# Band attention with its FFN on one core: values transposed by DMA, four engines' orders rewritten

## The reference

```python
xn  = layernorm(x)                                  # x: (8, 1024, 512)
Q, K, V = xn @ Wq + bq, xn @ Wk + bk, xn @ Wv + bv  # 16 heads of 64
scores  = Q K^T; scores = where(|i - j| <= 64, scores, 0.0)
attn    = softmax(scores, axis=-1)                  # over all 1024 columns
out = attn @ V @ Wo + bo
s = xn @ Win + bin_; h = relu(s[..., None] * W1 + b1)      # 64 units, 16 inner
g = sum(h * W2, -1) + b2; ffn = g @ Wout + bout
x + out + ffn
```

## Time and profile before

| | |
|---|---|
| median of 3 runs | 2254.79 us (2249.35 to 2255.46) |
| profiled execution | 2249.37 us, span 2247.6 us |
| mean granted TensorE clock | 0.953 |
| PE, PEld busy | 1994.0, 1110.4 us |
| DVE, ACT, POOL busy | 1754.1, 1473.2, 1399.4 us |
| DMA transposes | 512, all from SP's queue |

### The profile page before, as it was taken

One profiled execution on the slowest core, in us unless ns is written; L12 is line 12 of the kernel. 1 busy time (PEld: TensorE's weight loads), 2 busy tenths in 40 slices (PEclk: granted clock), 3 DMA queues, 4 the chain that ended last, 5 costly groups with the idle time before them and its releaser, 6 DMA issues.

```text
span 2247.6 us, 41992 instructions
## 1 busy us (share of the span) xinstructions
PE 1994.0 (89%) x14211; PEld 1110.4 (49%) x14211; DVE 1754.1 (78%) x4579; ACT 1473.2 (66%) x3961; POOL 1399.4 (62%) x1504
## 2 busy tenths in 40 slices
PE   7778888899889998899998999989989899889996
PEld 4444454555445554555454555545554555444553
DVE  5899877897678876888767887688776897677875
ACT  4767666667657675667666675657756667657664
POOL 3645547566577665667647665667747566577565
PEclk8889899999999999999999999999999999999998
DMA  3554435545365443555436545365445555354455
GB/s 120 129 125 98 104 91 116 138 104 113 71 139 131 103 97 78 141 127 112 95 76 148 113 102 109 72 173 108 96 80 115 138 105 113 70 138 96 91 102 118
DMA packets 610422, 247.01 MB, mean 110 GB/s; under 512 B 547336, under 2 KB 559648, under 8 KB 610208
## 3 DMA queue, kind: packets, MB, share of 16 engines
q1 hardware_dynamic: 610160, 244.30, 49.3%
q10 hardware_dynamic: 48, 0.01, 0.0%
HBM read 84.84 MB, written 25.17 MB: 49 GB/s over the span
## 4 chain that ended last, share of the span: by engine, by line
PE 36%; DVE 24%; ACT 20%; POOL 14%; issue 6%; DMA 0%; SPq 0%; ACTq 0%; DVEq 0%; POOLq 0%
PE ps L1128 16%; ACT probs L528 9%; POOL probs L386 8%; PE ps L1114 6%; ACT p_hi L584 6%; PE ps L1143 5%; DVE xn L901 4%; DVE acc L883 4%; DVE probs L851 4%; PE ps L1184 4%; POOL oT_lo L393 2%; POOL p_lo L399 2%; DVE row_l L863 1%; ACT qT_hi L576 1%; DVE vT L936 1%
## 5 line engine op out<-in xcount | busy, mean ns | idle before, releaser
L1128 PE MATMUL ps<-xT_hi,w_split 128*128 128x512 f16 x3072 | 985.7, 386 | 6.7 <-DVE xT_lo L739 6.4
L386 POOL TENSOR_SCALAR probs<-probs,inv_l,neg_e 128x256 f32<-128x256 f32 x1024 | 591.3, 597 | 290.4 <-DVE neg_e L870 290.2
L399 POOL TENSOR_TENSOR p_lo<-probs,p_hi 128x1024 f16<-128x1024 f32 x256 | 550.4, 2161 | 85.6 <-ACT p_hi L584 85.5
L1128 PE MATMUL ps<-xT_lo,w_split 128*128 128x512 f16 x1536 | 591.0, 385 | 0.0
L528 ACT ACTIVATE probs<-probs,neg_max 128x256 f32<-128x256 f32 x1024 | 505.2, 498 | 23.7 <-DVE neg_max L858 23.1
L1128 PEld LDWEIGHTS ps<-xT_hi,w_split 128*128 128x128 f16 x3072 | 304.2, 99 | 386.0 <-issue 30.4
L851 DVE CUSTOM_DVE_ANT_0 probs<-ps,mask,unit_s 128x256 f32<-128x256 f32 x1024 | 432.9, 477 | 43.8 <-PE ps L1114 43.8
L393 POOL TENSOR_TENSOR oT_lo<-o_sum,oT_hi 128x512 f16<-128x512 f32 x128 | 162.4, 1269 | 435.3 <-ACT o_sum L596 435.3
L584 ACT ACTIVATE p_hi<-probs 128x1024 f16<-128x1024 f32 x256 | 269.1, 1051 | 215.7 <-POOL probs L386 212.4
L883 DVE SCALAR_TENSOR_TENSOR acc<-ps,unit_o,acc 128x512 f32<-128x512 f32 x512 | 358.5, 740 | 18.6 <-PE ps L1143 18.5
L1143 PE MATMUL ps<-wo_split,oT_hi 128*128 128x512 f16 x1024 | 318.3, 394 | 53.8 <-DVE xT_lo L739 28.3
(11 more groups left out here) (119 smaller groups left out, 2969.2 us busy)
## 6 DMA issues: line engine op xcount, KB each, us to landing
w_split<-w_kept SPq DMA_DIRECT2D x168, 256.0 KB, 3.0
acc<-in_L_attn_x SPq DMA_DIRECT2D x14, 1024.0 KB, 7.0
out_x<-acc SPq DMA_DIRECT2D x14, 1024.0 KB, 5.3
wo_split<-wo_kept SPq DMA_DIRECT2D x56, 256.0 KB, 2.9
w_kept<-w_split SPq DMA_DIRECT2D x24, 256.0 KB, 2.4
pT_hi<-p_hi SPq DMA_TRANSPOSE x256, 3.1
pT_lo<-p_lo SPq DMA_TRANSPOSE x256, 3.3
acc<-in_L_attn_x SPq DMA_DIRECT2D x4, 512.0 KB, 5.6
```

The costliest lines, as they stand in the source:

```text
L386: pool.tensor_scalar(probs[:, h, t], probs[:, h, t], inv_l[:, c:c + 1], neg_e[:, c:c + 1], ALU.mult, ALU.add).then_inc(normed, 1)
L399: pool.tensor_tensor(p_split[lo][:, h, tiles], probs[:, h, tiles], p_split[hi][:, h, tiles], ALU.subtract).then_inc(p_lo, 1)
L1128: last = pe.matmul(dst[:], w[wp][:, i, c], xT[xp][:, c, half * LINE:half * LINE + LINE], start=(c == 0 and a == 0), stop=(c == KC - 1 and ...
```

## The change

V is no longer transposed on PE. ScalarE's `values_high` makes the fp16 high half of vT with the mean off (v_neg as its bias) into v_split, VectorE's `values_low` the low half, and SP's `transpose_values` brings both into v by two DMA transposes. The centring in place and the vT banks are gone, v is laid out by halves, and `value_means` also writes v_back. The orders of PE, DVE, ACT, POOL and SP change, the four low halves on POOL are four instructions each, and the banks are given out anew. The diff's core (eight columns of indentation left out):

```diff
 vT = sb("vT", [P, N])
-v = sb("v", [P, 2, T, 2, 2, D], F16)
+v_split = [sb(f"v_{part}", [P, N], F16) for part in ("hi", "lo")]
+v = sb("v", [P, 2, 2, T, 2, D], F16)
...
-V_BANK, VT_BANK = (3, 1), (6, 7)
+V_BANK = (6, 1)
 QK_BANK = (7, 2, 2, 3)
-OUT_BANK = (7, 0, 4, 5, 7, 0, 4, 5)
-PV_BANK = (6, 5)
-XT_BANK = (6, 0, 4, 1, 7, 0, 1, 6)
+OUT_BANK = (7, 0, 4, 5, 1, 0, 4, 5)
+PV_BANK = (6, 3)
+XT_BANK = (6, 7, 4, 5, 0, 1, 4, 5)
 FIRST_XT_BANK = (4, 5, 0, 2)
-FFN_IN_BANK = (6, 1)
-FFN_OUT_BANK = ((6, 3), (0, 1), (6, 4), (6, 3))
+FFN_IN_BANK = (6, 7)
+FFN_OUT_BANK = ((6, 3), (0, 1), (6, 7), (6, 3))
...
+TOP_BANK, LAST_TOP_BANK, FIRST_TOP_BANK, TOP_COLUMN = 1, 3, (1, 6), 32
 WARM_UP = 28
...
+    def transpose_values(n):
+        if n >= 2:
+            sp.wait_ge(pv_done, 2 * n - 2)
+        for part, ready in ((hi, v_hi), (lo, v_lo)):
+            sp.wait_ge(ready, n + 1)
+            sp.dma_start_transpose(v[:, n % 2, part].rearrange("p t h d -> p t (h d)"), v_split[part][:]) \
+                .then_inc(v_got, 16)
...
             load_x(b + 1, k - 2)
         if attend:
             transpose_weights(j, 0, 0, hi)
+            transpose_weights(j, 0, 0, lo)
             transpose_weights(j, 0, 1, hi)
-            transpose_weights(j, 0, 0, lo)
-            transpose_weights(j, 0, 1, lo)
         if k == 1 and b > 0 and proj:
             store(b - 1, 0)
         if proj:
             next_weights(V_)
+        if attend:
+            transpose_weights(j, 1, 0, hi)
+            transpose_weights(j, 0, 1, lo)
+        if proj:
             next_weights(Q_)
         if attend:
-            transpose_weights(j, 1, 0, hi)
             transpose_weights(j, 1, 1, hi)
         if proj:
...
         if attend:
             transpose_weights(j, 1, 0, lo)
             transpose_weights(j, 1, 1, lo)
+        if proj:
+            transpose_values(n)
         if n == PAIRS - 1:
...
         def weights_low(half, h):
-            tiles = slice(4 * half, 4 * half + 4)
             pool.wait_ge(p_hi, 4 * j + 2 * half + h + 1)
-            pool.tensor_tensor(p_split[lo][:, h, tiles], probs[:, h, tiles], p_split[hi][:, h, tiles],
-                               ALU.subtract).then_inc(p_lo, 1)
+            for t in tiles_of(half):
+                last = pool.tensor_tensor(p_split[lo][:, h, t], probs[:, h, t], p_split[hi][:, h, t],
+                                          ALU.subtract)
+            last.then_inc(p_lo, 1)
         def add_biases(p):
...
             normalise_weights(0)
-        if n <= PAIRS:
+        if n < PAIRS:
             inverse_root(tops_of_step(n), top_ready, scaled_in(n), root_ready)
         if attend:
             weights_low(0, 0)
-            weights_low(0, 1)
         if out_proj:
             output_low(1)
         if k == 0 and proj:
...
         if n == 0:
             add_biases(2)
             add_biases(3)
+        if k == 5 and not last:
+            inverse_deviation(slice(0, T), b + 3)
+        if attend:
+            normalise_weights(1)
+            weights_low(0, 1)
+            weights_low(1, 0)
+            weights_low(1, 1)
+        if n == PAIRS:
+            inverse_root(tops_of_step(n), top_ready, scaled_in(n), root_ready)
         if k == 1 and proj and b > 0:
             add_biases(2)
-        if k == 5 and not last:
-            inverse_deviation(slice(0, T), b + 3)
-        if attend:
-            normalise_weights(1)
-            weights_low(1, 0)
-            weights_low(1, 1)
-        if k == 1 and proj and b > 0:
             add_biases(3)
...
-        def values_high(i):
-            act.wait_ge(v_T, 2 * n + i + 1)
-            act.activation(v[:, n % 2, 4 * i:4 * i + 4, :, hi, :].rearrange("p c h d -> p (c h) d"),
-                           ps[VT_BANK[i]][:].rearrange("p (c d) -> p c d", d=D), ACT.Copy).then_inc(v_hi, 1)
+        def values_high():
+            act.wait_ge(v_stat, 3 * n + 3)
+            if n > 0:
+                act.wait_ge(v_got, 32 * n)
+            act.activation(v_split[hi][:], vT[:], ACT.Identity, bias=v_neg[:]).then_inc(v_hi, 1)
...
             for i in (Q_, K_, V_):
                 weights_top(n + 1, i)
+        hidden_high(0)
+        if ffn and k == 5:
+            network_high()
...
         if ffn and k == 0:
             x_high(b, 5)
-            x_high(b, 6)
         if attend:
             exps(3)
         if ffn and k == 0:
+            x_high(b, 6)
             x_high(b, 7)
-        if proj:
-            value_lines(0)
-        if attend:
-            weights_high(0, 1)
         if out_proj:
             weighted_sums(1)
-        hidden_high(0)
-        if ffn and k == 5:
-            network_high()
+        if proj:
+            value_lines(0)
+        if attend:
+            weights_high(0, 1)
         if ln_next and k == 6:
             normalise(b + 1, 2)
             normalise(b + 1, 3)
+        hidden_high(1)
         if proj:
             value_lines(1)
         if ln_next and k == 7:
             x_high(b + 1, 0)
         if ffn and k == 0:
             gather(0)
-        hidden_high(1)
+        hidden_high(2)
         if split_next:
             split_high(n + 1, V_)
         if ln_next and k == 7:
             x_high(b + 1, 1)
+        if proj:
+            values_high()
         if attend:
             weights_high(1, 0)
         if proj:
             qk_high(2)
         if split_next:
             split_high(n + 1, Q_)
-        hidden_high(2)
-        if ln_next and k == 6:
-            normalise(b + 1, 4)
-            normalise(b + 1, 5)
+        hidden_high(3)
         if attend:
...
             split_high(n + 1, K_)
-        if proj:
-            values_high(0)
-            values_high(1)
         if ln_next and k == 5:
...
         if ln_next and k == 7:
             normalise(b + 1, 6)
             normalise(b + 1, 7)
-        hidden_high(3)
...
-        def centre_values():
+        def value_means():
             dve.wait_ge(v_in, 2 * n + 2)
             dve.tensor_tensor(v_mean[:, 0:1], v_sums[:, 0:1], v_sums[:, 1:2], ALU.add).then_inc(v_stat, 1)
             dve.wait_ge(v_stat, 3 * n + 1)
             dve.tensor_tensor(v_mean[:, 1:2], v_mean[:, 0:1], v_sums[:, 2:3], ALU.add).then_inc(v_stat, 1)
             dve.wait_ge(v_stat, 3 * n + 2)
-            dve.tensor_scalar(v_new[:], v_mean[:, 1:2], 1.0 / N, None, ALU.mult).then_inc(v_stat, 1)
+            if n > 0:
+                dve.wait_ge(v_hi, n)
+            dve.tensor_scalar(v_neg[:], v_mean[:, 1:2], -1.0 / N, None, ALU.mult).then_inc(v_stat, 1)
             dve.wait_ge(v_stat, 3 * n + 3)
-            dve.tensor_scalar(vT[:], vT[:], v_new[:], None, ALU.subtract).then_inc(v_centered, 1)
-        def values_low(i):
-            part = [v[:, n % 2, 4 * i:4 * i + 4, :, p, :].rearrange("p c h d -> p (c h) d") for p in (hi, lo)]
-            dve.wait_ge(v_hi, 2 * n + i + 1)
-            dve.tensor_tensor(part[lo], ps[VT_BANK[i]][:].rearrange("p (c d) -> p c d", d=D), part[hi],
-                              ALU.subtract).then_inc(v_lo, 1)
+            if out_proj:
+                dve.wait_ge(o_summed, 2 * o + 2)
+            if n < PAIRS:
+                dve.wait_ge(bias_ready, k + 1)
+            dve.tensor_tensor(v_back[:, n % 2:n % 2 + 1], bias_scaled[:, V_, k:k + 1], v_neg[:], ALU.subtract) \
+                .then_inc(v_back_ready, 1)
+        def values_low():
+            dve.wait_ge(v_hi, n + 1)
+            dve.scalar_tensor_tensor(v_split[lo][:], vT[:], v_neg[:], v_split[hi][:],
+                                     ALU.add, ALU.subtract).then_inc(v_lo, 1)
...
+        if o > 0:
+            add_output(6, o - 1)
+            add_output(7, o - 1)
+        if 0 < j <= PAIRS:
+            split_output_low(j - 1)
+        if attend:
             mask_scores(1)
             mask_scores(2)
             denominators(0)
...
             qk_low(1)
-        if n <= PAIRS:
+        if ffn and k == 0:
+            x_low(b, 5)
+        if n < PAIRS:
             read_tops(tops_of_step(n), TOP_BANK, top_sum, scaled_in(n), top_ready)
         if ffn and k == 0:
-            x_low(b, 5)
             x_low(b, 6)
+        if ffn and k == 5:
+            network_low()
+        hidden_unit(0)
         row_statistics(0)
         if ln_next and k == 5:
             mean_and_variance(range(T), T * b + 2 * T, b + 3)
-        if attend:
-            denominators(1)
-        if n <= PAIRS:
-            step_scales(n)
         if ffn and k == 0:
             x_low(b, 7)
+        if attend:
...
             add_output(0)
             add_output(1)
         if ffn and k == 7:
             add_network(3)
-        hidden_unit(0)
         row_statistics(1)
-        if ffn and k == 5:
-            network_low()
+        if out_proj:
+            add_output(2)
...
         if ffn and k == 6:
-            add_network(0)
-        if out_proj:
-            add_output(2)
-            add_output(3)
-        if proj:
-            centre_values()
+            add_network(1)
+        if proj:
```

(94 more changed lines are left out.)

143 lines of the change are left out of this document (63 added, 80 removed).

## The result

The changed kernel takes 2305.85 us (median of four runs, 2302.93 to 2308.8) beside 2254.23 for the kernel before: a ratio of 1.0233, 95% interval 1.0211 to 1.0255. It is 2.3% slower, where 9% faster was forecast. The profiled execution has a span of 2301.2 us at a mean granted clock of 0.923. Every time given here is of a fast execution, except that the profile of e9_past_waits is of one of 2340.79 us in the slow state, which is left out of its times.

What follows compares the result with a forecast made beforehand. The prediction took middle steps as bound by PE plus a few waits, the first batch by DVE. Gains of 152 us (six middle batches), 33 (first) and 17 (last), together 202, gave 2050 us, range 1975 to 2165.

Steps and rivals of the forecast that it cites:

- plus 0.3 for each step of DVE waiting for POOL: Term of the middle-batch sum: DVE waits for POOL 0.3 us in each step, 2.4 us a batch.
- rival three: POOL's 11 us run of norm(1) and three low halves holds DVE's SBUF operations: 288 us, time 2335; chance 0.09.
- PE's 69 us: Value transposes and their waits leave PE: 1.08 us for each of 64 steps, 69 us.
- PE's idle time: Sign that the forecast is right: PE busy near 1920 us with some 120 us idle.
- 244.5 us: Forecast length of a middle batch's eight steps, for 269.8 us before: a gain of 25.3, times six 152.
- DVE's 80 us: Centring and two PSUM subtractions go, one 1.4 us update comes: about 80 us of DVE freed, 1.25 a step.
- Rival one: POOL shuts DVE's value sums out and values_high waits: 2.8 us every second step, 90 us, time 2140; chance 0.14.
- POOL's quarters: Low halves as four instructions of 0.56 us each on POOL, adding 0.4 us a step.
- a gain of some 33: First batch, bound by DVE: steps of 34.5 us against 39.2 for five, about 3 for each other three.
- Orders of PE: PE's new order removes most of the 4.9 us idle in k=7 and 3.9 in k=0; signs near 33 and 36.
- The remaining wait for kT_lo: At each step's end PE waits 0.35 us for kT_lo, whatever else is freed; 2.8 us a middle batch.
- Rival two: Late low halves on POOL delay PE's first weighted sums: 1.6 us a step, 102 us, time 2150; chance 0.14.

Runs made afterwards that it cites:

- e9_past_waits: e1_gaps with every GpSimd wait moved to the instruction before the last, so it is already met: ratio 1.0251 to the kernel before.
- e1_gaps: Changed kernel with GpSimd waiting for its own last instruction ahead of each low-half quarter and each bias instruction: 2126.22 us, 0.9451 of the kernel before.
- e7_before_gaps: Kernel before with only GpSimd's own-semaphore waits ahead of each whole low half and each bias instruction: 2185.36 us, ratio 0.9684.
- e5_gaps_keepq: Changed kernel with both edits, the GpSimd waits of e1_gaps and the SP order of e4_keepq: 2101.46 us, ratio 0.9315.
- e8_before_quarters: Kernel before with only each low half cut into four instructions, no waits between: 2348.3 us, ratio 1.0396.
- e11_gaps_early_swap: e10_gaps_early with SP's transpose of low half (0,1) also ahead of the (1,0) high one: 2164.75 us, ratio 0.9622.
- e12_pairs: e5_gaps_keepq with each low half in two pieces of 128x512 instead of four, a wait between each two: 2086.05 us, ratio 0.9267.
- e4_keepq: Changed kernel with SP issuing Q's store and next load ahead of transposes (1,0,hi) and (0,1,lo) in the first batch: 2273.46 us, ratio 1.0105.
- A and D: Two losses the experiments tested: A, DVE's SBUF instructions held through POOL's unbroken run (e1_gaps); D, SP's order in the first batch (e4_keepq).
- e10_gaps_early: e5_gaps_keepq with weights_low(0,1) moved back ahead of norm(1): 2165.97 us, ratio 0.964.
- e6_wgaps_keepq: e5_gaps_keepq with each low half one whole instruction instead of four quarters: 2135.0 us, ratio 0.9468.

## Why the prediction was wrong

**The step that failed** is the term "plus 0.3 for each step of DVE waiting for POOL", with the reason given against rival three: that most operations find a way between norm's short instructions, "and the low halves now come in such lengths". The same sum had put POOL's norm and low halves in one unbroken run of 11 us, and rival three named its place, hidden_unit(2) ahead of qk_low(3). It was given 0.09. Held over 2 us, DVE had 30 instructions in the kernel before (117 us), 67 after (278 us), none in e1_gaps. What e1_gaps gave back is 180 us, 2.8 us a step where 0.3 was taken: short of the 4.5 that the rival was priced at and near its point of decision, 3.2. A microsecond held is not a microsecond of time: 278 us of holds taken away gave 180, and 117 in the kernel before gave 70 (e7_before_gaps).

Of the 256 us between 2050 and 2306, then, 180 are this term, 25 SP's order (e5_gaps_keepq against e1_gaps), and 51 are left, 56 by the profiled executions. By the steps of e5_gaps_keepq they lie in the 48 middle ones (1503.6 us, where the sum had 1619.9 less 152) with 36, in the first batch with 18 and in the last with 5; the start and the tail give 3 back.

What misled was a reading of the median in the earlier trace rows: 0.80 for the centring beside a longest of 5.03. It was taken as what one meets between short instructions. It shows how DVE fares beside norm; at the joint of two low halves the row below it, 4.21 us of L399 x2, already showed a joint at which DVE didn't get in. e8_before_quarters is the test that would have settled it: more joints without a true wait are only a longer run.

**How long a hold lasts.** The 5.03 us was held against the sentence of the Trainium skill, "SBUF — State Buffer", section "SBUF: two separate sides", that the shared pair is locked for one whole instruction. The measurements go further: 11.93 us through more than ten instructions. They agree with the page where POOL truly waits between two (e1_gaps, at most 1.17 us in the same line), and at nearly all joints of norm's instructions (below).

**PE's 69 us**: busy time fell by 59.4 at a granted clock that fell from 0.953 to 0.923, while PE's idle time grew from 253.6 to 366.6 us. With the long waits gone (e1_gaps, clock 0.971) it is 117.6 less than before, part of it the clock's. In e11_gaps_early_swap, at 0.949, nearly the clock of before, it is 71.8 less. Right in size.

**PE's idle time** was to fall to some 120 us. It is 249.6 in e1_gaps, 222.3 in e5_gaps_keepq and 205.4 in e12_pairs, and 219.8 in the kernel before with waits alone (e7_before_gaps). So even undisturbed the change takes work off PE and hardly any waiting; that the middle batches come near their 244.5 us all the same (250.6 in e5_gaps_keepq) is in part a higher clock, 0.978 for 0.953, which the sum had not counted on. That part is luck.

**DVE's 80 us**: 104.5 more instead. In e1_gaps, where nothing is held long, busy time is 162.7 below the kernel before, twice what was taken, as the old holds went too. values_low was taken at 1.4 us:

```profile
L965 DVE SCALAR_TENSOR_TENSOR v_lo<-vT,v_neg,v_hi x64: 1268/1628/5293, 47.6 to 2255.7; 128x1024 f16<-128x1024 f32 x64
```

Its shortest, 1.27, is the lower bound, its longest, 5.29, a little past the upper one; in e1_gaps the median is 1296 ns. The size was right, the company wrong.

**ACT** was costed at nothing beside the wait for value_means. values_high takes 1.15 us (1.05 taken), and its wait for v_neg is 138.4 us, 73.5 in e5_gaps_keepq. Rival one (priced 90) is not what makes it: only 3 of the 64 first value sums are over 2 us longer than the shortest (7 us in all), and half of the wait is there where nothing is held long. Mostly ScalarE waits because DVE comes to the sums late; what that costs in time no run shows.

**POOL's quarters**: 0.56 us taken. In the run above they take 7.56 / 12 = 0.63, on average 0.69. All low halves together went from 550.4 to 672.1 us, 1.9 a step where 0.4 was taken. norm(1), to start 2.7 us sooner, starts 1.2 us sooner in k=4 (20.5 us into the step at the median, 21.7 before).

**DMA and SP.** The values' transposes were rightly free: issue 1.28 us, landing 3.3 at the median, nobody waits. But the sum looked only at what is read from SP's queue late, not at what must be written early: w_kept's store in the first batch. It cost some 30 us (e4_keepq), on a batch from which a gain of some 33 was expected (five steps by 4.7 and 9).

**Orders of PE.** k=7 "near 33" came (33.4), and k=0 at 33.6, better than the 36. k=4, forecast at 28 to 29, took 31.4 in the batch shown and up to 36.2 in others; in e1_gaps it is at 29.2. The remaining wait for kT_lo, taken as 0.35 us a step, has a median of 0.41 us in e1_gaps outside the first batch (33.6 us in 55 times), and 62.2 us in 8 times within it.

**Rival two** was right but hidden. With A and D gone PE waits 85.7 us for the late low halves, near the 102 it was priced at, and more than the 51 us between e5_gaps_keepq's 2101 and the 2050 forecast. Whether it makes that gap is not shown: the edit that takes the wait away costs more than it gives (e10_gaps_early), and pairs take part of it and make the wait for kT_lo longer.

Set against the kernel before with waits (2185), the change as made but for the joints (2126) is worth 59 us (52 by the ratios), and with SP's order 84. But the first has whole low halves and the others quarters. With whole ones in both, and SP's order (e6_wgaps_keepq, 2135.0), it is 50 us. So its value is real, but a quarter to two fifths of the 202 forecast even when nothing spoils it. Part of what was counted on, what the long holds of DVE cost, can be had without the change, as e7_before_gaps shows.

Open: why joints differ. Counting held DVE instructions (over 0.15 us longer than the shortest of their line and shape) at joints where POOL leaves no gap, in the kernel before they get in at all of the 63 joints between two norm instructions (one input) and at 14 of 43 between two low halves (two inputs); in the changed kernel at 91 of 98 and at 62 of 416. Whether it is the number of inputs or something else in these instructions wasn't tried; nor was the wait for pT_lo taken away without moving norm(1).

## What to carry to other kernels

Where VectorE's instructions with SBUF operands run beside GpSimd, look at the longest of a line, not at its median, and find out what GpSimd did in that time: a run of two-input instructions counts nearly as one, whatever it is cut into. A wait of GpSimd on its own last instruction opens each joint (here 3.2% on one kernel, 7.6% on the other, by 0.9451 / 1.0233), and then the pieces want a middle length. When transposes that wait for late data are put ahead of a store in an in-order queue, ask who waits for the buffer that the store frees.

## What the runs showed of the hardware

- An instruction of DVE of 0.74 us took 11.93 us beside some 15 instructions of POOL in a row, two-input ones of 0.63 and 1.2 us. Cutting the same work into four times as many pieces made a kernel 4% slower.
- A semaphore wait that is already met between two POOL instructions changes nothing (10.96 us still); one that must wait for the instruction before it limits the hold to about one piece: the longest hidden unit takes 1.17, 1.65 and 2.61 us with pieces of 0.74, 1.26 and 2.2 us.
- In the changed kernel a held DVE instruction got in at 62 of 416 unbroken joints of two 128x256 two-input instructions of POOL, and at 91 of 98 of two one-input instructions of the same size.
- The true wait costs POOL 0.12 us a joint at the median (0.63 to 0.75 us from start to start of quarters), 0.16 on average.
- Two DMA transposes of 128x1024 fp16 a step, with issue 1.28 and landing 3.3 us, ran beside eight others without being waited for.
